# Channel attention and integer FFN of a fused decoder, as one woven section with single banks

## The reference, cut to what matters

```python
x = _layernorm(x + _L0_xattn_ref(x, ctx, ctx), axis=-1)      # channel attention
x = _layernorm(x + _L0_ffn_ref(x, wq_gate, s_gate, wq_up, s_up, wq_down, s_down), axis=-1)

# channel attention: attends over the 256 channels, not over tokens
scaled = jnp.einsum('bsd,bse->bde', q, k) * scale
attn = jax.nn.softmax(scaled, axis=1)
out = jnp.einsum('bde,bse->bsd', attn, v)

# integer FFN, 256 -> 704 -> 256; each weight is (integer - 128) * a scale of its row
return _qlinear(silu(_qlinear(x, wq_gate, s_gate)) * _qlinear(x, wq_up, s_up), wq_down, s_down)
```

## Time and profile before

| | |
|---|---|
| time before, median of 3 | 4873.95 us (4869.34 to 4875.33) |
| the profiled execution | 4874.4 us, its span 4872.6 us |
| PE busy | 4443.3 us, 91% |
| DVE busy | 3285.7 us, 67% |
| ACT busy | 2040.9 us, 42% |
| POOL busy | 1523.5 us, 31% |
| mean granted TensorE clock | 0.967 of full |

### The profile page before, as it was taken

One profiled execution on the slowest core, in us unless ns is written; L12 is line 12 of the kernel. 1 busy time (PEld: TensorE's weight loads), 2 busy tenths in 40 slices (PEclk: granted clock), 3 DMA queues, 4 the chain that ended last, 5 costly groups with the idle time before them and its releaser, 6 DMA issues.

```text
span 4872.6 us, 87731 instructions
## 1 busy us (share of the span) xinstructions
PE 4443.3 (91%) x32645; PEld 3127.7 (64%) x32645; DVE 3285.7 (67%) x6084; ACT 2040.9 (42%) x4390; POOL 1523.5 (31%) x3050
## 2 busy tenths in 40 slices
PE   8998998799989888888699999999997999999788
PEld 6775887455546677777366666666664666666555
DVE  5667227788877688888655555555554676666798
ACT  4554113355544333333355555555552444444222
POOL 1111004434312233333344444444432333333222
PEclk9999999799999999999799999999998999999999
DMA  1003000444410200000000000000001000000000
GB/s 44 2 25 92 1 1 17 97 89 93 90 45 24 74 7 7 7 7 7 32 1 1 1 1 1 1 1 1 1 1 58 9 7 9 9 8 6 6 14 17
DMA packets 117700, 111.69 MB, mean 23 GB/s; under 512 B 22368, under 2 KB 110112, under 8 KB 112800
## 3 DMA queue, kind: packets, MB, share of 16 engines
q1 hardware_dynamic: 117280, 106.09, 8.4%
HBM read 88.48 MB, written 16.78 MB: 22 GB/s over the span
## 4 chain that ended last, share of the span: by engine, by line
PE 62%; issue 14%; DVE 13%; POOL 6%; ACT 2%; DMA 1%; SPq 1%; POOLq 0%; DVEq 0%; ACTq 0%
PE banks L2431 14%; PE banks L1918 5%; PE banks L1279 5%; PE banks L2681 4%; PE banks L769 4%; POOL factors L2893 3%; PE banks L1262 3%; PE banks L1155 2%; PE banks L1957 2%; PE banks L2497 2%; PE banks L798 2%; POOL mean_squares L2889 1%; PE banks L2597 1%; PE banks L523 1%; PE banks L2525 1%
## 5 line engine op out<-in xcount | busy, mean ns | idle before, releaser
L282 POOL TENSOR_TENSOR var_eps<-mean_var,ln_eps 128x1 f32<-128x1 f32 x384 | 75.4, 196 | 1031.0 <-DVE mean_var L278 961.9
L1319 ACT ACTIVATE exps<-banks 128x512 f32<-128x512 f32 x512 | 284.7, 595 | 219.3 <-PE banks L1262 219.3
L1167 DVE TENSOR_REDUCE neg_max<-banks 128x4 f32<-128x1024 f32 x256 | 309.5, 1211 | 86.8 <-PE banks L1155 86.6
L2452 ACT ACTIVATE squares<-banks 128x512 f32<-128x512 f32 x256 | 152.9, 597 | 440.3 <-PE banks L2431 440.3
L2485 DVE TENSOR_TENSOR q_normed<-banks,factors 128x512 f32<-128x512 f32 x256 | 176.3, 689 | 229.9 <-POOL factors L2475 229.9
L1918 PE MATMUL banks<-yT,w_swiglu 128*128 128x128 f32 x2048 | 274.7, 300 | 1.3 <-ACT yT L1902 1.3
L1918 PEld LDWEIGHTS banks<-yT,w_swiglu 128*128 128x128 f32 x2048 | 272.3, 218 | 1.6 <-ACT yT L1902 1.5
L2869 ACT ACTIVATE squares<-q_normed 128x512 f32<-128x512 f32 x160 | 100.8, 630 | 398.5 <-DVE q_normed L2859 398.5
L2475 POOL TENSOR_TENSOR factors<-mean_squares,minus_half 128x4 f32<-128x4 f32 x256 | 258.9, 1011 | 21.6 <-POOL mean_squares L2471 0.5
L2431 PE MATMUL banks<-wq,x_turned 128*128 128x512 f32 x512 | 248.9, 609 | 3.1 <-ACT x_turned L2411 1.9
L2681 PE MATMUL banks<-w_proj,yT 128*128 128x256 f32 x1024 | 242.2, 380 | 3.3 <-ACT yT L2664 3.2
(11 more groups left out here) (381 smaller groups left out, 11098.3 us busy)
## 6 DMA issues: line engine op xcount, KB each, us to landing
contextT<-in_ctxT SPq DMA_DIRECT2D x96, 128.0 KB, 2.5
parts_context<-parts SPq DMA_DIRECT2D x96, 64.0 KB, 2.5
parts_x<-parts SPq DMA_DIRECT2D x96, 64.0 KB, 2.0
stack<-parts_context SPq DMA_DIRECT2D x32, 192.0 KB
stack<-parts_x SPq DMA_DIRECT2D x32, 192.0 KB
x_all<-in_x SPq DMA_DIRECT2D x1, 4096.0 KB, 14.2
context<-in_ctx SPq DMA_DIRECT2D x64, 64.0 KB, 2.2
context<-in_ctx SPq DMA_DIRECT2D x32, 128.0 KB, 2.3
```

Source lines behind the costliest of these rows:

```text
L1167: v.tensor_reduce(self.mx[s][:, :, 2 * i:2 * i + 2].rearrange("p h g -> p g h"), self.bM[i % 2].rearrange("p g (h c) -> p g h c", h=DH), A ...
L1319: self.nc.scalar.activation(self.e[n % 8][:], self.bE[self.slot(t, n) % 2].rearrange("p (l c) -> p l c", l=DH), ACT.Exp, scale=self.TOK ** ...
```

## The change

Channel attention and the integer FFN become one section. Its step n holds channel attention's pieces for tiles n, n-1, ... and the FFN's pieces five steps later: tile n-5 is turned and goes through gate and up in the step in which tile n is scored. The FFN's turning of x becomes a piece of its own, first in PE's list, ahead of channel attention's weighing, the down matmuls, gate and up, and the score. Channel attention has one pair of score banks (4 and 5) and one output bank (6), the FFN keeps 0, 1 to 3 and 7. Six steps of the section are put into causal attention's end instead of ten, the weights (25.5 KB a partition) are loaded at the kernel's start, and five steps of shared head attention come before steps 38 and 39. As the count of sections is one less, the sides on which weights and work buffers lie swap from there on. One buffer of context attention (`wo`) is allocated first.

```diff
-        self.bS = (p.ps[:, 1:3, :], p.ps[:, 3:5, :]); self.bY = [p.bank[5 + s][:, 0:D] for s in (0, 1)]
+        self.bS, self.bY = p.ps[:, 4:6, :], p.bank[6][:, 0:D]
...
-    def leaves(self):
-        end = self.NT - 1
-        scored = {bank: self.exped.end(end - 1 + bank // 3) for bank in (1, 2, 3, 4)}
-        return {**scored, 5: self.summed.end(end - 1, 1), 6: self.summed.end(end, 1)}
...
-        if not begun(t - 2):
-            self.enter(pe, 1 + 2 * s, 2 + 2 * s)
+        if first(t):
+            self.enter(pe, 4, 5)
         else:
-            pe.wait_ge(self.exped.sem, self.exped.all(t - 2))
+            pe.wait_ge(self.exped.sem, self.exped.all(t - 1))
         for b in (0, 1):
             for e in range(DH):
-                last = self.nc.tensor.matmul(self.bS[s][:, b, e * D:(e + 1) * D], c[:, b, e * P:(e + 1) * P], self.p.x_all[:, t.index, :],
+                last = self.nc.tensor.matmul(self.bS[:, b, e * D:(e + 1) * D], c[:, b, e * P:(e + 1) * P], self.p.x_all[:, t.index, :],
                                              start=True, stop=True)
...
-        v.tensor_reduce(self.nm[s][:], self.bS[s].rearrange("p b (e d) -> p (b e) d", e=DH), AX.X, ALU.max, negate=True).then_inc(self.maxed.sem, 1)
+        v.tensor_reduce(self.nm[s][:], self.bS.rearrange("p b (e d) -> p (b e) d", e=DH), AX.X, ALU.max, negate=True).then_inc(self.maxed.sem, 1)
...
-        if not begun(t - 2):
-            self.enter(pe, 5 + s)
+        if first(t):
+            self.enter(pe, 6)
         else:
-            pe.wait_ge(self.summed.sem, self.summed.at(t - 2, 1))
+            pe.wait_ge(self.summed.sem, self.summed.at(t - 1, 1))
...
-        self.tail_sum(dve, t, s, self.bY[s])
-
-    def programs(self):
-        return {
-            "pe": [(3, self.weigh_pe), (0, self.score_pe)],
-            "act": [(1, self.exp_act)],
-            "dve": [(4, self.sum_dve), (1, self.max_dve), (2, self.normalise_dve), (4, self.tail_scale)],
-            "pool": [(4, self.tail_pool)],
-            "sp": [(0, self.p0_sp)],
-        }
+        self.tail_sum(dve, t, s, self.bY)
...
-    def p0_pe(self, pe, t, s):
+    def turn_x_pe(self, pe, t, s):
         if first(t):
             self.enter(pe, 0)
         self.head_pe(pe, t, s, self.bT)
+
+    def p0_pe(self, pe, t, s):
...
-    def programs(self):
+    @staticmethod
+    def behind(channel, own):
+
+        at = 5
         return {
-            "pe": [(2, self.p2_pe), (0, self.p0_pe)],
-            "act": [(1, self.p1_act), (0, self.p0_act)],
-            "dve": [(3, self.p3_dve), (1, self.p1_dve), (3, self.tail_scale)],
-            "pool": [(3, self.tail_pool)],
-            "sp": [],
+            "pe": [(at, own.turn_x_pe), (3, channel.weigh_pe), (at + 2, own.p2_pe), (at, own.p0_pe), (0, channel.score_pe)],
+            "act": [(at + 1, own.p1_act), (at, own.p0_act), (1, channel.exp_act)],
+            "dve": [(at + 1, own.p1_dve), (1, channel.max_dve), (at + 3, own.p3_dve), (4, channel.sum_dve), (2, channel.normalise_dve),
+                    (at + 3, own.tail_scale), (4, channel.tail_scale)],
+            "pool": [(at + 3, own.tail_pool), (4, channel.tail_pool)],
+            "sp": [(0, channel.p0_sp)],
...
+        self.wo = w("wo", [P, self.H, D])
...
-    (alone, (ChannelAttention,), 1, 1, (130, 133, 134, 135, 136, 137, 138, 139, 140, 141)),
-    (alone, (IntegerFFN,), 25, 25, (33, 34, 35)),
-    (alone, (SharedHeadAttention,), 21, 21, (33, 33, 34, 34, 34, 35, 35)),
+    (IntegerFFN.behind, (ChannelAttention, IntegerFFN), 25.5, 25.5, (133, 134, 135, 137, 138, 140)),
+    (alone, (SharedHeadAttention,), 21, 21, (38, 38, 39, 39, 39)),
...
-            side = 1 - side if starts else 0
+            side = 1 - side if starts else side
```

More of the change, by code:

```diff
@@ L658, in exp_act @@
             b, e = divmod(j, DH)
-            self.nc.scalar.activation(self.e[s][:, b, e, :], self.bS[s][:, b, e * D:(e + 1) * D], ACT.Exp, bias=self.nms[s][:, j:j + 1],
+            self.nc.scalar.activation(self.e[s][:, b, e, :], self.bS[:, b, e * D:(e + 1) * D], ACT.Exp, bias=self.nms[s][:, j:j + 1],
                                       scale=self.SCALE, accum_out=self.den[s][:, j:j + 1]).then_inc(self.exped.sem, 1)
@@ L678, in weigh_pe @@
         pe.wait_ge(self.cn_ready.sem, self.cn_ready.all(t))
-        if not begun(t - 2):
-            self.enter(pe, 5 + s)
+        if first(t):
+            self.enter(pe, 6)
         else:
-            pe.wait_ge(self.summed.sem, self.summed.at(t - 2, 1))
+            pe.wait_ge(self.summed.sem, self.summed.at(t - 1, 1))
         for e in range(DH):
             for b in (0, 1):
-                last = self.nc.tensor.matmul(self.bY[s][b * SEQ:(b + 1) * SEQ, :], self.cn[s][:, e, b * SEQ:(b + 1) * SEQ], self.e[s][:, b, e, :],
+                last = self.nc.tensor.matmul(self.bY[b * SEQ:(b + 1) * SEQ, :], self.cn[s][:, e, b * SEQ:(b + 1) * SEQ], self.e[s][:, b, e, :],
                                              start=(e == 0), stop=(e == DH - 1), skip_group_check=True)
@@ L2728, in __init__ @@
             self.load(self.w[kind][:], halves(p.ins["L3_xattn_W" + kind]))
-        self.wo = w("wo", [P, self.H, D])
         self.finish_loads()
```

## The result

The changed kernel takes **4972.84 us** (median of 4, 4969.44 to 4977.94) against 4873.93 us before (median of 4 now): ratio 1.0205, 95% interval 1.0188 to 1.0223, 98.9 us slower. The profiled execution has a span of 4976.2 us, 103.6 more than before. Forecast were 4920 and a range of 4898 to 4956. The direction and the wait were right; the size was not: the granted clock, which the sum took to fall in one full step of ten, fell in 22 of the 24.

The account below looks back on a forecast made before the run. TensorE, busy 91%, was the bound in the FFN, VectorE in channel attention; joined full steps wait on the single output bank. Profiled 4874.4 + 42.0 + 4 = 4920.4, median 0.45 below: 4920 us; own range 4905 to 4938, with rivals 4898 to 4956.

Parts of the forecast that it names:

- a chain that starts at the score just made: Full steps: score, reduction, scaling, FFN addition and statistics, channel addition precede weighing; 4.90 us, a 2.76 us stall, 13.75 us steps.
- The savings: TensorE waits the joining removes: 0.84 us a tile for xT, 6.9 for weight dequantising, 8.1 for one context transfer.
- a fall in one of ten steps: Full steps: TensorE's granted clock rarely falls behind the 2.49 us gap; 4 us in all, bounds 0 and 40.
- Rival A: Clock falls in most full steps, as with the 2.83 us gaps: 25 to 40 us more, about 4950; chance 0.18.
- 42.0 and 4: Forecast's two additions to the profiled time: 42.0 us later at the last down matmuls, 4 us for clock falls.
- to score(5): Section's start: first score at 331.8, later scores waiting for exponentials, sixth score at 370, 5 us either way.
- 24 full steps: Steps 8 to 31 at 13.75 us each, 330.0 us, from score(7) at 392.9 to score(31) at 722.9.
- score(31) to last down: Section's end: steps shrinking to 11.5 and 9.45 us, last gate and up at 778.5, last down matmuls at 790.1.
- B: Weighing is not late, the channel's sum comes in time; full steps are TensorE's 11.0 us, 4840 us; chance 0.07.
- C: The wait is shorter, 1.7 us, if the FFN's sum costs less before the channel's; 4891 us; chance 0.07.
- D: ScalarE's two table loads a step come onto the path: 64 us more, 4980 us; chance 0.03.
- D's own sign: In a full step, a table load followed by its first exponential later than 6.0 us would decide for D.

Follow-up runs that it names:

- The order experiments: Changed kernel with one list reordered: VectorE both sums before maximum, 4847.7 us; VectorE maximum, channel sum, FFN sum, 4902.7 us; TensorE weighing behind down matmuls, 4906.5 us.
- fill1: Changed kernel plus one unused filling matmul on TensorE in each step's wait for the residual: 4935.5 us.
- fill3: Changed kernel plus three unused filling matmuls on TensorE in each step's wait for the residual: 4931.6 us.
- sum_mid: Changed kernel with VectorE's order maximum, channel attention's sum, then the FFN's sum: 4902.7 us.
- tanh: Changed kernel with Tanh in place of Silu in the FFN, so ScalarE need not change tables: 4977.1 us.
- seam_pool: Changed kernel with VectorE's sums ahead of the maximum and context buffers cleared earlier by GpSimd: 4844.6 us; span 9.0 us under that without the early clearing.
- before_s1: Kernel before the change, with one pair of score banks and both output banks in channel attention: 4976.0 us.
- before_y1: Kernel before the change, with one output bank and both pairs of score banks in channel attention: 4874.6 us.

## Why the prediction was wrong

**Right: the bound and the chain.** "So weighing always waits for a chain that starts at the score just made": forecast 4.90 us and 13.75 a step, measured 4.81 and, at full clock, 13.88. The down matmuls take 2.69 us there and not the 2.49 of the sum. The order experiments, which take out terms of this chain, fell where their sums said. The savings came too: xT, w_down and the 8.1 us transfer are gone from the waits.

**Wrong: the clock.** The step that failed is "I take a fall in one of ten steps, 4 us, since 2.49 is nearer to 2.25". Two things were off. The gap is 2.71 us, not 2.49: the turning of x starts 1.72 us after the first score matmul (403.17 to 404.89), where I had added 1.92 and 0.11 (2.03), so the idle time begins 0.3 us sooner and the chain ends 0.1 sooner. And I placed the gap between a harmless 2.25, a single one, and a harmful 2.83 by its length alone. That does not hold: in these steps gaps of 2.27 us made the clock fall in three of 24 (3 x 1.69 = 5.1 us, 3.9 in the medians, whose ranges overlap, fill1 against fill3), gaps of 2.71 in 22 of 24 (44.7 us). Rival A, named with 0.18, is the mechanism that happened. Its price, 4941 to 4956 us, was still low: a step with a fall lost 2.0 us and not 1.6, and the start and the end lost more, as follows.

**Where the 105.1 us at the last down matmuls come from** (748.1 to 853.2), against the forecast 42.0 and 4:

| stretch | forecast | measured | |
|---|---|---|---|
| to score(5) | 370 | 380.0 | +10.0 |
| score(5) to score(7) | 22.9 | 23.2 | +0.3 |
| 24 full steps | 330.0 | 377.8 | +47.8 |
| score(31) to last down | 67.2 | 72.2 | +5.0 |

Behind that point the rest of the kernel was 1.5 us shorter, which leaves the 103.6 of the spans. Of the 47.8, 24 x 0.13 = 3.1 is the full step itself (down matmuls 0.20 longer, chain 0.09 shorter, the rest 0.02) and 44.7 the clock. Of the 10.0 at the start, 2.6 are the first score, at 334.35 and not 331.8, 0.9 come up to score(4), and 6.5 between score(4) and score(5), 16.54 us and not 10. In the timeline of the changed kernel:

```profile
334.35 3.75 PE L634 MATMUL banks<-x_all,context 128*128 128x256 f32 x8 [7.77 <-DMA contextT<-in_ctxT]
...
341.68 3.59 PE L634 MATMUL banks<-x_all,context 128*128 128x256 f32 x8 [3.27 <-ACT probs L654]
...
363.42 3.75 PE L634 MATMUL banks<-x_all,context 128*128 128x256 f32 x8 [2.16 <-ACT probs L654]
...
368.98 0.42 DVE L271 TENSOR_TENSOR residual<-banks,x_biased 128x256 f32<-128x256 f32 x1 [7.77 <-PE banks L556]
...
370.00 1.20 DVE L643 TENSOR_REDUCE neg_max<-banks 128x4 f32<-128x1024 f32 x1
...
371.88 1.62 PE L680 MATMUL banks<-probs,context_n 128*64 128x256 f32 x8 [2.72 <-DVE residual L271]
```

Scores at 334.35, 341.68 and 363.42 take 3.6 to 3.8 us and not 2.0. I had reckoned two of them so and let the clock recover for the rest; the granted clock was 0.73 from 363.42 to 379.96. A second term was missing there: VectorE's maximum stood behind causal attention's last addition, which waited for its output projection (L556) until 368.98, so weighing came 8.5 us after score(4) and not 4. The 5.0 at the end are the clock again: the step from 781.04 took 16.9 us and not 13.8, and one of the two steps with a wait of 2.12 us took 13.2 and not 11.5 (the clock was 0.52 from 812.5 to 816.0). The error in the clock stands in three places, then: a wait was priced as its length alone.

**The other rivals.** B (PE-bound, 4840) is what the kernel becomes with the sums ahead: its mechanism was absent and its price right within 8 us. C is sum_mid, 4891 forecast, 4902.7 measured. D did not occur, by tanh, but its argument was wrong and its rejection in part luck. The load did wait for what its exponentials wait for, and D's own sign, a first exponential later than 6.0 us into the step, was there: 403.17 to 410.43 is 7.3 us. It cost nothing because the next score comes 13.9 us into the step, long after the last exponential (412.4).

Still open: how much of seam_pool's 9 us is real, and what besides the length of a wait makes the clock fall.

## What to carry to other kernels

When two stages are woven, look in each engine's list for a piece that frees a buffer and stands behind a piece that waits for the newest result; here that order made one output bank cost a wait of 2.7 us in each step, and exchanging two entries of one list was worth 125 us. Price a wait of TensorE twice, once as its length and once as the clock behind it. If its length is near one that made the clock fall elsewhere in the same trace, give the fall in every period a full share of the chances, and compare how often the waits come, not only how long they are. A second buffer is worth what the other work in the step does not cover: a second pair of score banks 102 us when the stage stood alone, and no wait for it to save in the full steps of the woven form.

## What the runs showed of the hardware

- Of idle stretches of TensorE once in a full step of the woven section, those of 1.41 and 1.72 us left the clock at 1.00 throughout (fill3, sum_mid), 2.27 us let it fall in 3 of 24 steps (fill1), 2.71 us in each from the third on (changed; in tanh from the fifth). The cost was 44.7 us over 24 steps, of which the last 22 had the fall: some 2.0 us in each.
- The length alone does not decide: idle stretches of 2.18 us, once in 6.79 us, left a mean clock of 0.75 in every step (before_s1), while 2.27 us once in 13.88 us mostly left it at 1.00 (fill1).
- Filling 1.3 us of the 2.71 us of idle time in each step with useless matmuls made the kernel 41 us faster (fill3).
- A table load of ScalarE took 1.28 us, and the next function started 0.01 us behind it. The Trainium skill, ScalarE: Activation LUTs, section What ACT_TABLE_LOAD costs, gives 2.66 us with a drain; here no drain stood beside it. At 1.28 two loads a step were covered (tanh); at 2.66 Silu's would not have been there at 413.68, and what that would cost no run shows.
- "Adding PSUM double-buffering gave no further gain" (the Trainium skill, TensorE: Matmul & The Clock Gate, section HAM oscillation) is said there of one kernel for thin matrices. Here it held for the second output bank and not for the second pair of score banks: before_y1 lost nothing, before_s1 lost 102 us.
